# Double steps of attention with one shift product per row quarter, and context parts kept in DRAM, in a two-layer perceiver kernel

## The reference

```python
s = einsum('bhid,bhjd->bhij', q, k) * SCALE      # layer 0: 16 heads of 64, 256 queries, 4096 keys
p = softmax(s, axis=-1)
o = einsum('bhij,bhjd->bhid', p, v)
k, v = ctx @ Wk, ctx @ Wv                        # both layers project the same ctx (4096 x 192)
```

## Time and profile before

| | us |
|---|---|
| median of 3 runs | 2086.76 (2086.05 to 2088.25) |
| the profiled execution, its own time | 2086.96 |
| its span in the profile | 2085.3 |
| PE busy | 1888.4 (91%) |
| PEld busy | 1269.3 (61%) |
| DVE busy | 1096.4 (53%) |
| ACT busy | 1031.0 (49%) |
| POOL busy | 650.1 (31%) |

### The profile page before, as it was taken

One profiled execution on the slowest core, in us unless ns is written; L12 is line 12 of the kernel. 1 busy time (PEld: TensorE's weight loads), 2 busy tenths in 40 slices (PEclk: granted clock), 3 DMA queues, 4 the chain that ended last, 5 costly groups with the idle time before them and its releaser, 6 DMA issues. The chain is left out here.

```text
span 2085.3 us, 33327 instructions
## 1 busy us (share of the span) xinstructions
PE 1888.4 (91%) x13464; PEld 1269.3 (61%) x13464; DVE 1096.4 (53%) x1550; ACT 1031.0 (49%) x1363; POOL 650.1 (31%) x315
## 2 busy tenths in 40 slices
PE   6899999999899999999999776868998999766999
PEld 2576766667566676666766544448544844443887
DVE  3577586675665767667562244247100800374565
ACT  1244444444554444444442232116897799625443
POOL 1026565555544656556564212002000100010000
PEclk9899999999999999999999888788999999977999
DMA  5510000000300000000020100004463355400220
GB/s 185 142 46 6 6 16 1 16 6 6 97 1 16 6 6 16 1 16 6 1 74 7 61 0 1 18 15 112 74 105 66 81 92 97 107 1 1 92 97 35
DMA packets 89922, 90.59 MB, mean 43 GB/s; under 512 B 29928, under 2 KB 79824, under 8 KB 86448
## 3 DMA queue, kind: packets, MB, share of 16 engines
q1 hardware_dynamic: 88736, 87.46, 17.3%
q10 hardware_dynamic: 1040, 1.05, 0.2%
HBM read 58.57 MB, written 8.91 MB: 32 GB/s over the span
## 5 line engine op out<-in xcount | busy, mean ns | idle before, releaser
L760 POOL TENSOR_TENSOR sums<-sums,probs 128x1024 f32<-128x1024 f32 x224 | 534.7, 2387 | 354.8 <-ACT probs L793 305.1
L844 DVE TENSOR_REDUCE part_max<-psum_banks 128x2 f32<-128x1024 f32 (+1 forms) x256 | 312.8, 1224 | 125.8 <-PE psum_banks L1006 121.3
L793 ACT ACTIVATE probs<-psum_banks 128x1024 f32<-128x1024 f32 x240 | 245.9, 1024 | 123.2 <-PE psum_banks L1052 116.0
L1066 PE MATMUL psum_banks<-probs,values 128*64 128x256 f32 x2048 | 278.4, 393 | 0.3 <-ACT probs L796 0.3
L771 ACT ACTIVATE keys<-psum_banks 64x512 fp32r<-64x512 f32 x256 | 151.6, 592 | 239.0 <-PE psum_banks L979 235.9
L2472 ACT ACTIVATE probs<-psum_banks,k_inv_norm 128x1024 f32<-128x1024 f32 x256 | 257.9, 1260 | 1.3 <-PE psum_banks L2487 1.2
L837 DVE TENSOR_TENSOR keys<-psum_banks,keys 64x512 fp32r<-64x512 f32 x256 | 176.4, 689 | 116.8 <-ACT keys L771 110.8
L1066 PEld LDWEIGHTS psum_banks<-probs,values 128*64 128x64 f32 x2048 | 124.5, 136 | 99.8 <-issue 60.1
L1034 PEld LDWEIGHTS psum_banks<-q_hi,keys 128*128 128x128 f32 x1024 | 138.0, 189 | 76.7 <-issue 51.7
L1034 PE MATMUL psum_banks<-q_hi,keys 128*128 128x256 f32 x1024 | 184.6, 302 | 0.0
L776 ACT ACTIVATE values<-psum_banks 128x512 f32<-128x512 f32 x128 | 76.5, 598 | 192.7 <-PE psum_banks L991 192.7
(11 more groups left out here) (443 smaller groups left out, 3036.3 us busy)
## 6 DMA issues: line engine op xcount, KB each, us to landing
k_pairs<-keys SPq DMA_DIRECT2D x192, 128.0 KB, 4.2
ctx_tok<-in_ctx SPq DMA_DIRECT2D x16, 384.0 KB, 3.5
wk_pair<-wkv_parts SPq DMA_DIRECT2D x16, 256.0 KB, 3.0
wv_quad<-wkv_parts SPq DMA_DIRECT2D x8, 512.0 KB, 3.8
w_gate_up<-in_L_ffn_gate_proj_w SPq DMA_DIRECT2D x8, 512.0 KB, 4.0
w_gate_up<-in_L_ffn_up_proj_w SPq DMA_DIRECT2D x8, 512.0 KB, 5.0
w_down<-in_L_ffn_down_proj_w SPq DMA_DIRECT2D x8, 512.0 KB, 5.9
ctx_tok_b<-in_ctx SPq DMA_DIRECT2D x8, 384.0 KB, 5.2
```

The lines of the kernel that those rows point to most:

```text
L760: pool.tensor_tensor(sums[:, :, :, :], probs[:, 0, :, :, :] if step == 1 else sums[:, :, :, :], probs[:, step % SLOTS, :, :, :], ALU.add). ...
L793: act.activation(probs[:, step % SLOTS, :, :, :], scores, ACT.Exp, scale=SCALE0).then_inc(p_ready, 1)
L844: dve.tensor_reduce(part_max[:, :, i, c], psum[:, bank:bank + 2, 0:width], AX, ALU.max).then_inc(m_read, 1)
L1066: last = pe.matmul(psum[rows(h), 3, 0:L], values[:, kt, at:at + HD0], probs[:, step % SLOTS, h, j, :], start=kt == 0, stop=kt == KT - 1, t ...
```

## The change

**Double steps.** The loop of layer 0's attention goes over 8 double steps in a unit. PE's order in one is: keys of a later unit; `begin_scores` of the next two steps; one `shift_scores` for both; `finish_scores` of both; the first block of maxima; `weigh` of two steps; in the last one `denominators`; `spread_maxima`; the second block of maxima; values, two pieces (or `turn_a` and `turn_b`) together. The second piece goes to bank 1, and the spread maxima go to bank 0; waits follow from a list for each of the two banks.

**Shift products.** `shift_scores` is four products of 32 rows, one in each row quarter of the array and each into one of the banks 4 to 7, in place of two products of 64 rows in each of the two steps. The quarters 0 and 2 hold the first head's shift, 1 and 3 the second's, and the shift is the maximum over 32.

**Other engines in layer 0.** POOL makes a 16th addition in a unit (128 x 512, both halves of `sums`), and `denominators` has two products instead of four. `high_queries` moves from DVE to ACT. The reciprocal is cut in four quarters, in four double steps, after every odd unit (all at once after even ones); `low_queries` for odd units run both in one double step, the last of the unit before the one before.

**Context parts.** SP writes `cA_hi`, `cA_lo` and `cB` to DRAM (three DMAs of 2 MB for each batch: for the first one ahead of the loop, for the second one at m = 10). In layer 1 SP loads them in chunks (three DMAs of 256 KB) into four slots; turning and splitting fall away. The key pairs' DMAs are issued ahead of the loads of chunks 6 and 7.

```diff
 class Core:
+        self.context_parts = nc.dram_tensor("ctx_parts", (B, 3, P, N), F32, kind="Internal").ap()
...
+TWOS = STEPS // 2
+def keys_at(m, c):
+    return (m - 1) * TWOS + c - 2
+def spread_at(m):
+    return m * TWOS - 2
+def high_queries_at(m, h):
+    return (m - 2) * TWOS + 1 + h
+def low_queries_at(m, h):
+    return (m - 1) * TWOS + (3 + h if m % 2 == 0 else -1)
+def pieces_of_double_steps():
+    ahead, top, behind = ({g: [] for g in range(FIRST, END)} for _ in range(3))
+    for m in range(1, UNITS):
+        for c in range(CHUNKS):
+            g = max(keys_at(m, c), FIRST)
+            if (m, c) != (1, 0):
+                ahead[g].append(("keys", m, c))
+            for i in range(2):
+                top[g].append(("max", m, c, i))
+    for c in range(CHUNKS):
+        behind[(PAIRS - 2) * TWOS + c] += [("turn_a", 0, c), ("turn_b", 0, c)]
+    for quad in range(1, UNITS // 2):
+        for c in range(TWOS):
+            behind[(2 * quad - 1) * TWOS + c] += [("values", quad, 2 * c), ("values", quad, 2 * c + 1)]
+    return ahead, top, behind
...
+                def keep_parts(b):
+                    for i, part in enumerate((cA_hi, cA_lo, cB)):
+                        sp.dma_start(core.context_parts[b, i, :, :], part[:, :].bitcast(F32)).then_inc(parts_kept[b], 16)
                 widen_second()
+                keep_parts(0)
...
                         pool.tensor_tensor(sums[:, :, :, :], probs[:, 0, :, :, :] if step == 1 else sums[:, :, :, :],
                                            probs[:, step % SLOTS, :, :, :], ALU.add).then_inc(summed, 1)
+                    pool.wait_ge(summed, n * SUMS + STEPS - 1)
+                    pool.tensor_tensor(sums[:, :, 0, :], sums[:, :, 0, :], sums[:, :, 1, :], ALU.add).then_inc(summed, 1)
...
                 def shift_scores(m, step):
-                    bank = 4 + 2 * (step % 2)
                     if step == 0:
                         pe.wait_ge(shift_ready, m + 1)
-                    for h in range(2):
-                        pe.matmul(psum[:, bank + h, :], ones_r[rows(h), :],
-                                  shift[rows(h), m % 2, None, :].to_broadcast([HD0, 2, L]), start=False, stop=False)
+                    for r in range(4):
+                        pe.matmul(psum[:, 4 + r, :], ones_r[quad_rows(r), :],
+                                  shift[quad_rows(r), m % 2, None, :].to_broadcast([QUAD, 2, L]), start=False, stop=False,
+                                  tile_position=(QUAD * r, 0))
...
+                for g in range(FIRST, END):
+                    next_two = (2 * g + 2, 2 * g + 3) if g < END - 1 else ()
+                    for piece in ahead[g]:
                         prepare(piece)
+                    if g >= END - TWOS:
+                        output_part(2 * (g % TWOS))
+                    for step in next_two:
+                        begin_scores(step // STEPS, step % STEPS)
+                    for step in next_two[:1]:
+                        shift_scores(step // STEPS, step % STEPS)
+                    for step in next_two:
+                        finish_scores(step // STEPS, step % STEPS)
                     for piece in top[g][:1]:
                         prepare(piece)
                     if g >= 0:
+                        for step in (2 * g, 2 * g + 1):
+                            weigh(step // STEPS, step % STEPS)
+                        if g % TWOS == TWOS - 1:
+                            denominators(g // TWOS)
+                    for m in range(1, UNITS):
+                        if g == spread_at(m):
+                            spread_maxima(m)
                     for piece in top[g][1:]:
                         prepare(piece)
                     for piece in behind[g]:
                         prepare(piece)
+                    if g >= END - TWOS:
+                        output_part(2 * (g % TWOS) + 1)
...
 def l1x_keys_values(core, b, s, keys, values, inv_norm, k_ready):
+                for c in range(CHUNKS):
+                    if c >= SLOTS:
+                        sp.wait_ge(v_done, 2 * (c - SLOTS + 1))
+                    for i, part in enumerate((cA_hi, cA_lo, cB)):
+                        sp.dma_start(part[:, c % SLOTS, :].bitcast(F32),
+                                     core.context_parts[b, i, :, c * CHUNK:(c + 1) * CHUNK]).then_inc(arrived[c % SLOTS], 16)
+                    if c == SLOTS + 1:
+                        if b == 0:
+                            sp.wait_ge(pairs_padded, 2)
+                        sp.wait_ge(k_hi, CHUNKS * 2)
+                        sp.wait_ge(k_lo, CHUNKS * 2 + 4)
+                        load_key_pairs(sp, s, keys, 0, 0, k_ready)
```

More of the change, by code:

```diff
@@ L634, in l0_attention @@
     QW = 4 * HD0
+    QUAD = P // 4
     PASSES = ((0, cA_hi), (1, cA_hi), (0, cA_lo), (2, cB), (3, cB))
-    SUMS = STEPS - 1
+    SUMS = STEPS
+    QUARTERS = 4
     SLOTS = 4
     Q_SLOTS = 3
-    first, second, top, behind = steps_of_pieces()
-    in_bank0 = [("keys", 1, 0)] + [p for g in range(FIRST_STEP, LAST_STEP) for p in first[g] + second[g] + behind[g]]
-    before_in_bank0 = dict(zip(in_bank0, [("keys", 0, CHUNKS - 2)] + in_bank0))
+    ahead, top, behind = pieces_of_double_steps()
+    in_bank0 = [("keys", 0, CHUNKS - 2), ("spread", 0), ("keys", 1, 0)]
+    in_bank1 = [("max", 0, CHUNKS - 1, 0)]
+    for g in range(FIRST, END):
+        in_bank0 += ahead[g] + [("spread", m) for m in range(1, UNITS) if g == spread_at(m)] + behind[g][:1]
+        in_bank1 += top[g] + behind[g][1:]
+    previous = {**dict(zip(in_bank0[1:], in_bank0)), **dict(zip(in_bank1[1:], in_bank1))}
     wide = nc.dram_tensor("ctx_second_wide", (N, 2 * P), F32, kind="Internal").ap()
@@ L660, in l0_attention @@
         tok_in = [sem(f"ctx_tok_in{i}") for i in range(4)]
+        parts_kept = [sem(f"ctx_parts_kept_b{b}") for b in range(B)]
         q_hi_ready, q_lo_ready = sem("q_hi_ready"), sem("q_lo_ready")
@@ L797, in weights, with high_queries @@
                                        scale=SCALE0, bias=last_bias[:, :]).then_inc(p_ready, 1)
+                def high_queries(m, h):
+                    q = qT[:, m % PAIRS, m // PAIRS * L:(m // PAIRS + 1) * L]
+                    for half in range(2):
+                        act.activation(q_hi[rows(half), m % Q_SLOTS, h, :], q[rows(h), :], ACT.Copy).then_inc(q_hi_ready, 1)
+                for h in range(2):
+                    high_queries(0, h)
                 act.wait_ge(consts, 2)
@@ L801, in _ @@
                     prepare(piece, alone=True)
+                for h in range(2):
+                    high_queries(1, h)
                 prepare(("keys", 1, 0))
-                for g in range(FIRST_STEP, LAST_STEP):
-                    for piece in first[g] + second[g]:
+                for g in range(FIRST, END):
+                    for piece in ahead[g]:
                         prepare(piece)
-                    if g < LAST_STEP - 1:
-                        weights((g + 1) // STEPS, (g + 1) % STEPS)
+                    if g < END - 1:
+                        for step in (2 * g + 2, 2 * g + 3):
+                            weights(step // STEPS, step % STEPS)
                     for piece in behind[g]:
                         prepare(piece)
-                    if g == LAST_STEP - STEPS + 8:
+                    for m in range(2, UNITS):
+                        for h in range(2):
+                            if g == high_queries_at(m, h):
+                                high_queries(m, h)
+                    if g == END - TWOS + 4:
                         act.wait_ge(o_turned, 9)
@@ L914, in _ @@
                 dve.memset(ones_r[:, :].bitcast(F32), 1.0).then_inc(out_kept, 1)
-                for m in range(2):
-                    for h in range(2):
-                        high_queries(m, h)
                 for h in range(2):
@@ L2362, in _ @@
             def _(dve):
-                dve.sem_inc(c_lo, 2)
                 dve.sem_inc(k_lo, 4)
```

284 lines of the change are left out of this document (100 added, 184 removed).

## The result

| | before | after |
|---|---|---|
| median of 4 runs each, us | 2087.51 (2086.05 to 2089.07) | 2035.74 (2030.50 to 2038.34) |
| the profiled execution, its own time | 2086.96 | 2036.46 |
| its span | 2085.3 | 2034.7 |
| mean granted clock of that execution | 0.950 | 0.937 |

The ratio is 0.9749, with a 95% interval of 0.9728 to 0.9770: 52 us less. The forecast was 2006, 81 us less. The time lies in the prediction's wide range, 1978 to 2048, but outside the range of its main forecast, 1988 to 2030.

A forecast was written before the change was run, and what follows sets the result against it. The prediction took PE's instruction list to bound layer 0's attention. Savings of 24 (even units), 44 (odd), 0, 0 and 13 (layer 1) sum to 81 us, from 2086.96 to 2006; main range 1988 to 2030, wide 1978 to 2048.

The forecast's parts named there:

- The change of rows is free: Rival, shift block: going from 32-row to 64-row products costs nothing, 24 us less, 1984; chance 0.09.
- Two quarters at a time: Rival, shift block: only two row quarters run together, 0.46 for the four products, 29 us more, 2035; chance 0.05.
- The quarters run one after another: Rival, shift block: four products run serially, 0.69 more in each of 128 double steps, 88 us, 2094; chance 0.05.
- two terms for the shift block: Double step: four quarter products save 0.23 us; the new change from 32 to 64 rows is priced at 0.2.
- this costs nothing or nearly so, with no cover to spare: Odd units, bank 1: PE reaches the second values piece within 0.1 us of the end of the second maxima's reading.
- I call it even, 0: Unit 0: a gain of 3.8 us is offset by three waits of 1.77 between four blocks of maxima.
- Zero: Unit 15: about 4 us saved, offset by output parts 2, 4, 6 and 8 each waiting about 1.1.
- done 0.6 before `denominators` asks: POOL, end of a unit: the 16th addition, 1.2 us, finishes 0.6 before PE needs it.
- 13: Layer 1's keys and values: stored parts save about 6.5 us a batch, twice, after a 2.5 wait at chunk 6.
- The stored parts bring nothing: Rival, layer 1: loads and key pairs share one queue, chunks 6 and 7 arrive late, 13 us gone, 2019; chance 0.09.
- DVE's order: Rival, second maxima: DVE reads the first maxima late in each double step, 48 us more, 2054; chance 0.12.
- signs of being wrong: Layer 0 units: wrong if an even unit stays above 50 us, or waits on DVE exceed 2 us in a unit.

The follow-up runs named there:

- e8: Changed kernel with each of the four quarter shift products issued twice, with half the shift: 2059.86 us in one run.
- e2: Kernel before, in single steps, with its two shift products cut from 64 to 32 rows: 2134.64 us, ratio 1.0220.
- e1: Changed kernel with double steps kept, but the four shift products back to 64 rows in row halves: 2036.51 us, ratio 0.9746.
- e9: Changed kernel with only the second values piece moved to the next double step, behind its begin_scores and keys; turn_b stays: 2021.94 us, ratio 0.9692.
- e6: Changed kernel with unit 1's extra maxima blocks spread over three double steps and its queries' high parts made at the start: 2031.50 us, ratio 0.9735.
- e11: Changed kernel with e4, e6, e7, e9, unit 1's queries split at the start, and no 16th addition in unit 15: 2006.50 us, ratio 0.9608.
- e7: Changed kernel with unit 15's output parts 1, 3, 5 and 7 put ahead of weighing: 2029.76 us, ratio 0.9719.
- e12: As e11, but unit 1's extra maxima are not spread; four blocks stay in the first double step: 2008.98 us, ratio 0.9628.
- e3: Changed kernel with layer 1's context turned and split anew as before the change, and no parts written to DRAM: 2045.01 us, ratio 0.9783.
- e4: Changed kernel with layer 1's key-pair DMAs issued after the loads of all chunks: 2023.82 us, ratio 0.9686.
- e5: Changed kernel with every second piece, values and turn_b, moved to the next double step behind its begin_scores and keys: 2037.02 us, ratio 0.9750.

## Why the prediction was right in direction and 30 us off

**Double steps: right.** An even unit gives 48.8 against 48.7. The four quarters side by side, 0.23, is shown by e8, and the price of 0.2 for a change from 32 to 64 rows by e2. Neither "The change of rows is free" nor "Two quarters at a time" nor "The quarters run one after another" holds. The prediction's two terms for the shift block, 0.23 saved and a change of shape spent, nearly cancel; it did not say so, and e1 shows it. The gain comes from pairing the steps, which puts products of like shape together: with halves a double step has four changes of shape for six in two single steps, 0.4 at 0.2 each, and 6.32 less e1's double step of 5.98 (411.95 to 417.93), 0.34, came (0.37 with quarters).

**"this costs nothing or nearly so, with no cover to spare"** is the step that failed in the odd units. The wait for bank 1 costs 0.24 in a double step, 1.9 in a unit, where 1.5 a unit had been left for waits of all kinds; with the 0.06 that every double step is longer than forecast, an odd unit takes 69.4 instead of 68.5. In unit 6, whose two pieces were priced "as before", the wait was 0.9 for each `turn_b`, so that unit gained nothing:

```profile
PE psum_banks L1047 <- DVE part_max L865: 5.9, 7, 1.6
```

e9 shows the price in the odd units by taking the wait away: 1.4 in an odd unit, 10 of its 14 us.

**"I call it even, 0" for unit 0** was 9.0 wrong. The waits of a block, 1.77, were right (starts 1.86 to 2.16 apart, of which the products cover some); what was left out is that the keys ahead of them wait too, and that the clock then drops, so that the work behind the pauses runs at half speed. e6 removes the pauses and gets one of DVE's instead; e11 keeps the clock and takes 7.2 off.

**"Zero" for unit 15** was 4.8 wrong, in part for the same reason. Four waits of 1.1 were forecast; they are printed at 0.8 to 1.8, and the clock fell behind the longest. The longer fall among the products of 8 columns was not forecast either, and its cause stays open. e7, which separates the parts, gives 5.4 of trace time and 6 of median. Another 2.0 of the 4.8 is the longer wait for POOL at the unit's end, which the forecast had put at nothing ("done 0.6 before `denominators` asks"). In e11 and e12, without the 16th addition there, that wait is 2.2 instead of 3.5; what it costs was not tried alone.

**Layer 1, "13"**, is mis-sized: 7 in the trace, 7 to 9 by e3. The 5.6 for seven turns came (7 x 0.86 = 6.0). The delay at chunk 6, forecast at 2.5 in each batch, measured 5.2 in the first and 8.6 in the second, waits and lower clock together. The mechanism was seen (SP's queue in order, key pairs ahead of the loads) but it was taken as given; e4 shows that it was the larger part of what layer 1 had to give, 12 us. The rival "The stored parts bring nothing" had this mechanism and too high a price.

**DVE's order**: the rival named it at 48 us, at the second maxima of each double step. There it did not come. But the reductions hold PE elsewhere: 4.3 between the blocks of unit 0, 5.9 at `turn_b` in unit 6, and, printed nowhere, 0.24 in 56 double steps with values, 13. That is about 23 in all, so the mechanism was real at half its price. Of the prediction's own signs of being wrong, the even unit (48.8) stays below 50, but waits on DVE make up more than 2 us in unit 0 and in unit 6.

**What unit 0, unit 15 and layer 1 share** is that a wait was priced at its length. By the mean clock, time at 1.2 GHz is 2 x (1 - 0.950) x 2085 = 209 us before and 2 x (1 - 0.937) x 2035 = 256 after. In the 48 more, PE does half of what it could, which is up to 24 us; some of that time is idle in any case, so this is an upper bound. The waits themselves are the rest, with no claim to completeness: unit 15's second fall has no pause ahead of it.

## What to carry to other kernels

Count a PE program in changes of array shape as well as in columns: packing products into smaller tiles pays only when it saves more than the change of shape (0.2 us here) that it brings, and here the gain lay in putting like shapes together. Price a pause of PE at a stage's edge with the slow stretch behind it, not only at its own length, and put independent work between two users of one bank. On one DMA queue, put first what is wanted first: 12 small copies in each batch ahead of two loads cost 12 us here, where the stored parts themselves were worth 7 to 9.

## What the runs showed that was not expected

- **Executions differ more after the change.** The kernel before stays within 3 us in four runs (within 6 in the nine beside e9 to e12), and the kernel after within 8 in four; e11 ran from 1998.5 with a mean clock of 0.947 to 2014.8 with 0.938. That step of 0.009 is 2 x 0.009 x 2006 = 36 us at half clock, worth up to 18 of PE's time, about the 16 seen. How often the clock drops differs between executions of the same program: unit 15 of the same code took 76.0 to 82.2 in the profiled executions of the kernels that leave it alone. What decides it was not found.
- **Four products in row quarters cost what two in row halves cost**, at 512 columns each: 0.24 for the four (e8), 0.23 for the two.
- **A pause can be absent from the idle column.** The 0.24 at bank 1 stands in the double steps with values and in no row of the waits; the distance between starts is the only place to read it.
- **Moving the pause is not removing it.** e5 and e6 both took a wait away as meant, and DVE's next instruction in order made a new one.
